# A two-layer metaformer kernel: one pass over a quadrant's similarity, seeds and inverse norms in place of two half passes

## The reference, cut to what matters

```python
x = x + _L0_conv_ref(_ln_c(x), ...)
# in _L0_conv_ref, for each quadrant (64 x 64 tokens) and head (4 heads of 24 channels):
sim = sigmoid(sim_beta + sim_alpha * einsum('bmc,bnc->bmn', _l2norm(ctr), _l2norm(pts)))
idx = argmax(sim, axis=1)                 # over the 4 centres, the first of equals
mask = (arange(M)[None, :, None] == idx[:, None, :])
sim = sim * mask
agg = (einsum('bmn,bnc->bmc', sim, value2) + value_centers) / (sum(sim, axis=-1) + 1.0)
out = einsum('bmc,bmn->bnc', agg, sim)    # then a 1x1 projection
```

## Time and profile before

| | |
|---|---|
| median of three runs | 3819.1 us |
| profiled execution | 3818.97 us |
| its span, first to last instruction | 3817.1 us |
| TensorE matmul busy, whole span | 2982.5 us (78%) |
| VectorE busy | 3196.7 us (84%) |
| ScalarE busy | 2886.1 us (76%) |
| POOL busy | 1726.6 us (45%) |
| mean granted TensorE clock, as a share of 2.4 GHz | 0.905 |

### The profile page before, as it was taken

How to read it: one execution, slowest core, us unless ns; L and a number is a source line. 1 busy time by engine, 2 the same in 40 slices (tenths; PEclk the granted TensorE clock), 3 DMA queues, 4 the chain that set the end, 5 groups by cost and what they waited for, 6 DMA issues and landing times. The chain is left out here.

```text
span 3817.1 us, 67552 instructions
## 1 busy us (share of the span) xinstructions
PE 2982.5 (78%) x21476; PEld 1982.1 (52%) x21476; DVE 3196.7 (84%) x8114; ACT 2886.1 (76%) x6562; POOL 1726.6 (45%) x2404
## 2 busy tenths in 40 slices
PE   5777777777777777777766999998878778778787
PEld 5556565656556565656543555554444444444443
DVE  4888888888888888888884899888898898889887
ACT  2577777777777777777776666665799999999998
POOL 3777777777777777777751000000221212221221
PEclk7798888888888888888876999999899999999999
DMA  2232323323332323333214777796666666666762
GB/s 59 59 84 68 84 68 84 84 76 84 76 84 67 84 68 84 81 79 85 59 52 130 216 219 220 220 281 177 162 184 190 171 176 192 187 169 175 195 178 67
DMA packets 708503, 484.58 MB, mean 127 GB/s; under 512 B 407068, under 2 KB 686940, under 8 KB 696156
## 3 DMA queue, kind: packets, MB, share of 16 engines
q1 hardware_dynamic: 708156, 480.27, 47.0%
HBM read 278.37 MB, written 201.33 MB: 126 GB/s over the span
## 5 line engine op out<-in xcount | busy, mean ns | idle before, releaser
L1834 POOL TENSOR_SCALAR C_var<-C_st 128x16 f32<-128x16 f32 x64 | 16.8, 263 | 1463.9 <-DVE C_st L175 1463.9
L1415 DVE SCALAR_TENSOR_TENSOR B_y<-B_mid,B_coefs,B_y 128x512 f32<-128x512 f32 x768 | 521.5, 747 | 77.4 <-ACT B_y L1382 77.4
L1333 PE MATMUL B_ps_row<-B_z,B_g 128*128 128x512 f32 x1152 | 520.1, 601 | 0.0
L375 DVE TENSOR_SCALAR A_hq<-A_h,A_b 128x512 f16<-128x512 f16 x768 | 292.5, 417 | 237.7 <-ACT A_h L367 230.7
L367 ACT ACTIVATE A_h<-A_hid 128x512 f16<-128x512 f32 x768 | 427.8, 593 | 63.4 <-PE A_hid L354 60.1
L175 DVE BATCH_NORM_STATS2 A_st<-A_xT 128x6 f32<-128x192 f32 x1536 | 443.3, 350 | 27.1 <-ACT A_xT L831 13.2
L367 ACT ACTIVATE C_h<-C_hid 128x512 f16<-128x512 f32 x768 | 426.7, 593 | 15.8 <-PE C_hid L354 8.6
L1455 ACT ACTIVATE C_q<-C_xT,C_shift,C_rstd 128x96 fp8e5<-128x96 f32 x1024 | 392.4, 458 | 30.7 <-POOL C_shift L1841 30.7
L861 ACT ACTIVATE A_xc<-A_xT,A_shift,A_rstd 128x96 f32<-128x96 f32 x1024 | 380.0, 459 | 0.0
L164 POOL TENSOR_TENSOR A_rstd<-A_var,A_expo 128x16 f32<-128x16 f32 x128 | 374.6, 2927 | 10.7
L668 PEld LDWEIGHTS A_fbank<-A_big_w,A_xq 97*128 97x128 f32 x2048 | 318.1, 225 | 29.2 <-issue 11.1
(11 more groups left out here) (160 smaller groups left out, 7325.8 us busy)
## 6 DMA issues: line engine op xcount, KB each, us to landing
A_xq<-in_x SPq DMA_DIRECT2D x32, 1536.0 KB, 8.9
x_scratch<-A_xT SPq DMA_DIRECT2D x64, 768.0 KB, 3.2
x_scratch<-A_x3h SPq DMA_DIRECT2D x64, 768.0 KB, 5.4
B_z<-x_scratch SPq DMA_DIRECT2D x96, 512.0 KB, 4.2
y_scratch<-B_y SPq DMA_DIRECT2D x96, 512.0 KB, 5.3
C_x3q<-x_scratch SPq DMA_DIRECT2D x32, 1536.0 KB, 9.1
C_xT<-x_scratch SPq DMA_DIRECT2D x64, 768.0 KB, 15.5
C_y3q<-y_scratch SPq DMA_DIRECT2D x31, 1536.0 KB, 15.5
```

What stands on the lines that cost most here:

```text
L375: r = dve.tensor_scalar(self.hq[:, b, s], self.h16[:, b, s], self.w["b1"][:, j:j + 1], 0.0, ALU.add, ALU.max)
L1333: m = pe.matmul(bank(c, h), g[c.buf(2)][:, d, :], z[c.buf(NB)][:, half(h), d:d + W], start=(d == 0), stop=(d == 2))
L1415: dve.scalar_tensor_tensor(y, mid[c.buf(2)][:, half(h), t:t + W], coefs[:, c.n, 3 + t:4 + t], y, ALU.mult, ALU.add).then_inc(ev["sums"], 1)
```

## The change

All of the quadrant's similarity is done at once. `cosines`, the sigmoid and `similarity` each run once for 128 x 128 (or 512) elements, in slots 5 and 6; the two transposes stand in slots 7 and 8; the seeds and the Newton steps run once, behind slot 3, with `pool_norm(i, 3)` ahead of them; `scaled_sim` runs once. The sums of squares are taken for two blocks at a time. The tie buffer becomes part of `eq`, whose rows grow from 4 to 9 floats: the running maximum of the marks stands in columns 0, 4 and 8, so the first copy falls away. `projected` writes its four diagonal blocks with one product by a mask of ones (`own_block`, four new columns of the constants).

```diff
-COS_AT = {3: 0, 5: 1}
-SIM_AT = {4: 0, 6: 1}
-SIMT_AT = {5: 0, 7: 1}
+COS_AT, SIM_AT = 5, 6
+SIMT_AT = {7: 0, 8: 1}
...
-        eq = sb("A_eq", [P, NT * HEADS, M], F32)
-        taken = sb("A_taken", [P, NT * HEADS, M - 1], F32)
+        eq = sb("A_eq", [P, NT * HEADS, M + (M - 2) * M - M + 1], F32)
...
-                pe.wait_ge(ev["sim"], ev.at("sim", q, h))
+                pe.wait_ge(ev["sim"], ev.at("sim", q, 0))
...
-                    act.wait_ge(ev["n2"], ev.at("n2", q, c - NSQ))
+                    act.wait_ge(ev["n2"], ev.at("n2", q, (c - NSQ) // 2))
...
-                        act.activation(sim[:, t, :], dots[:, t, :], ACT.Sigmoid, scale=ab[:, 0:1],
+                        act.activation(sim[:], dots[:], ACT.Sigmoid, scale=ab[:, 0:1],
...
-            def norms(q, c):
+            def norms(q, pair):
+                c = 2 * pair
-                dve.wait_ge(ev["big"], ev.at("big", q, c))
-                dve.tensor_reduce(n2[:, c * HM:(c + 1) * HM], sq[:, c % NSQ].rearrange("p t (h d) -> p (t h) d", d=HD),
+                dve.wait_ge(ev["big"], ev.at("big", q, c + 1))
+                dve.tensor_reduce(n2[:, c * HM:(c + 2) * HM],
+                                  sq[:, c % NSQ:c % NSQ + 2].rearrange("p k t (h d) -> p (k t h) d", d=HD),
                                   AX_X, ALU.add).then_inc(ev["n2"], 1)
...
-            def similarity(q, h):
+            def similarity(q):
...
-                dve.wait_ge(ev["eq"], ev.at("eq", q, h))
-                dve.tensor_copy(taken[:, u, 0], e[:, :, 0]).then_inc(ev["tie"], 1)
+                dve.wait_ge(ev["eq"], ev.at("eq", q, 0))
                 for m in range(1, M - 1):
-                    dve.wait_ge(ev["tie"], ev.at("tie", q, (M - 1) * h + m - 1))
-                    dve.tensor_tensor(taken[:, u, m], taken[:, u, m - 1], e[:, :, m], ALU.max).then_inc(ev["tie"], 1)
+                    if m > 1:
+                        dve.wait_ge(ev["tie"], ev.at("tie", q, m - 2))
+                    dve.tensor_tensor(eq[:, :, M * m], eq[:, :, M * (m - 1)], e[:, :, m], ALU.max).then_inc(ev["tie"], 1)
...
-                dve.tensor_tensor(e[:, :, 1:M], e[:, :, 1:M], taken[:, u, :], ALU.is_gt).then_inc(ev["only"], 1)
+                dve.tensor_tensor(e[:, :, 1:M], e[:, :, 1:M], eq[:, :, 0:M * (M - 2) + 1:M], ALU.is_gt).then_inc(ev["only"], 1)
...
-                for t in range(TPC):
-                    g = slice(32 * t, 32 * t + 32)
-                    m = dve.tensor_scalar(pabd[g, t * C:(t + 1) * C], s_pa[g, 0:C], rden[g, :], None, ALU.mult)
-                m.then_inc(ev["pabd"], 1)
+                dve.scalar_tensor_tensor(pabd[:].rearrange("p (t c) -> p t c", c=C),
+                                         s_pa[:, 0:C].unsqueeze(1).to_broadcast([P, TPC, C]), rden[:],
+                                         own_block.unsqueeze(2).to_broadcast([P, TPC, C]),
+                                         ALU.mult, ALU.mult).then_inc(ev["pabd"], 1)
...
-                for h in range(2):
-                    if q2.real:
-                        inverse_norms(q2, h)
-
-                        pool.wait_ge(ev["rn"], ev.at("rn", q2, h))
-                    if i.real and h == 0:
-                        ff.pool_norm(pool, i, 3)
+                if i.real:
+                    ff.pool_norm(pool, i, 3)
+                if q2.real:
+                    inverse_norms(q2)
                 if i.real:
                     ln3(i, 0)
-                if q2.real:
-                    scaled_sim(q2, 0)
                 if q1.real:
                     ln2(q1, 0)
...
                 if q2.real:
-                    scaled_sim(q2, 1)
+                    scaled_sim(q2)
```

More of the change, by code:

```diff
@@ L467, in phase_a @@
                     xT=NK, bn1=NK, ln1=2, ln1_s=4, pooled=1, cf=1, cfc=1, csq=1, cn2=1, cn2c=1, cpow=1, chat=1,
-                    c16=1, cw=1, cwc=1, big=NK, n2=NK, n2c=2, seed=2, rn_s=22, rn=2, guarded=2, cos=2, sig=2, mx=2, eq=2,
-                    tie=6, only=2, sim=2, simr=2, simT=2, side=1, sided=1, pool=1, agg=1, gathered=2, sum=1, summed=1, val=1,
+                    c16=1, cw=1, cwc=1, big=NK, n2=NK // 2, n2c=1, seed=1, rn_s=11, rn=1, guarded=1, cos=1, sig=1, mx=1, eq=1,
+                    tie=M - 2, only=1, sim=1, simr=1, simT=2, side=1, sided=1, pool=1, agg=1, gathered=2, sum=1, summed=1, val=1,
                     rden=1, aT4=1, pa=1, pabd=1, bn3=NK,
@@ L986, in cosines @@
[L986 to L992, removed]
+            def norms(q, pair):
[3 more added lines that the diff above has]
+                                  sq[:, c % NSQ:c % NSQ + 2].rearrange("p k t (h d) -> p (k t h) d", d=HD),
+                                  AX_X, ALU.add).then_inc(ev["n2"], 1)
+                if c + 2 == NK:
+                    dve.wait_ge(ev["n2"], ev.at("n2", q, pair))
+                    dve.tensor_scalar(n2c[:], n2[:], TINY, None, ALU.max).then_inc(ev["n2c"], 1)
+                    dve.wait_ge(ev["n2c"], ev.at("n2c", q, 0))
+                    dve.tensor_scalar(seed[:].bitcast(U32), n2c[:].bitcast(U32), -0.5, SEED_BITS, ALU.mult,
+                                      ALU.add).then_inc(ev["seed"], 1)
@@ new lines, in similarity @@
+                    dve.tensor_tensor(eq[:, :, M * m], eq[:, :, M * (m - 1)], e[:, :, m], ALU.max).then_inc(ev["tie"], 1)
+                dve.wait_ge(ev["tie"], ev.at("tie", q, M - 3))
+                dve.tensor_tensor(e[:, :, 1:M], e[:, :, 1:M], eq[:, :, 0:M * (M - 2) + 1:M], ALU.is_gt).then_inc(ev["only"], 1)
+                dve.wait_ge(ev["only"], ev.at("only", q, 0))
+                dve.tensor_tensor(sim32[:, :, 0:HM].rearrange("p t (h m) -> p t h m", m=M),
+                                  sim[:].rearrange("p t (h m) -> p t h m", m=M),
+                                  e.rearrange("p (t h) m -> p t h m", h=HEADS), ALU.mult).then_inc(ev["sim"], 1)
@@ L1061, in body @@
                         own_heads(q1)
-                    if q2.real and s in COS_AT:
-                        cosines(q2, COS_AT[s])
+                    if q2.real and s == COS_AT:
+                        cosines(q2)
                     if i.real and s < NK:
                         ff.dve_hidden(dve, i, s)
-                    for c in BIG_AT.get(s, ()):
-                        if q2.real:
-                            norms(q2, c)
+                    if q2.real and s in BIG_AT:
+                        norms(q2, s)
                     if i.real and s >= 1:
@@ L1085, in body @@
                         projected(q1)
-                    if q2.real and s in SIM_AT:
-                        similarity(q2, SIM_AT[s])
+                    if q2.real and s == SIM_AT:
+                        similarity(q2)
                     if q2.real and s == AGG_AT:
@@ L1886 @@
         consts[32 * t:32 * t + M, K_QUARTERS:K_QUARTERS + M] = np.eye(M, dtype=np.float32) / np.float32(2 * CH)
+    for t in range(TPC):
+        consts[32 * t:32 * t + 32, K_BLOCK + t] = 1
     consts[0:C, K_CEN:K_CEN + C] = np.eye(C, dtype=np.float32) - np.float32(1 / C)
```

76 lines of the change are left out of this document (31 added, 45 removed).

## The result

The changed kernel takes 3893.9 us (median of three runs, 3893.5 to 3895.6), the kernel before 3819.9 us beside it: a ratio of 1.0193, interval 1.0176 to 1.0210. A fourth run took 9402 us, a slow state that one later run of the kernel before shows too (6261 us); it counts in no number here. The change is slower by 74 us, where I had forecast 3822 us and a range up to 3848 us. The profiled execution took 3893.5 us, its span is 3891.7 us and the mean granted clock 0.882.

What follows compares the result with a forecast made beforehand. No one engine bounds the step throughout, though VectorE leads; -1.85 us (stretches A and B) and +1.9 (C) give +0.05 a step, 1.5 in 30 steps, plus 2 for filling: 3822 us from 3818.97, range 3790 to 3848.

Steps and rivals of the forecast that it cites:

- The mechanism: Bank order makes the gather's 64 matmuls wait for block 5's eviction, starting 2.04 us later; similarity once a step, about 3.5 us.
- One of its signs: Expected in the changed trace: VectorE's wait for the hidden copy grows by about what its busy time falls.
- Stretch C: Slot 8 to slot 1, a chain over all engines: the later gather makes it +1.9 us a step.
- I take half the steps at either level: Gather's clock: half the steps at 2.4 GHz, half at 1.2 GHz, so 7.58 - 5.67 = +1.9 us a step.
- Stretch A: Slots 2 to 4, ScalarE busy throughout: one sigmoid leaves, 0.5 us a step gained; VectorE's savings there worth nothing.
- Stretch B: From VectorE's wait for ScalarE's hidden copy to the end of slot 7's rounding: VectorE's savings count in full, -1.35 us a step.
- slots 0 to 1: The step's first two slots, from the first hidden copy to ScalarE's first copy of `y`: no size of their own forecast.
- The rival with the gather at half clock in every step: Gather at 1.2 GHz each time: +2.64 us from slot 8 on, step loses 0.79, 3845 us; chance 0.22.
- half clock that lasts into the next step's slot 0: TensorE's lower clock continuing past the hidden copy: left outside the range, with no size given.
- Filling the pipeline: Two quadrants pass with nothing beside them, longer instructions on the path: +2 us in all, bounds -2 and +6.
- the norm pairs and the masked product: VectorE's norm sums and `projected`, where ScalarE bounds: savings hidden, taken as nothing; norm pairs -0.2 to +0.2 us a step.
- POOL's Newton steps in a row: Twelve instructions of 128 elements, about 6.4 us between seeds and cosines with 9.5 us left: hidden, by 3 us.

Runs made afterwards that it cites:

- e1: The changed kernel with both transposes of the similarity in slot 7, so the gather no longer waits for block 5's eviction: 3772.1 us.
- e3: The changed kernel with 28 unread transposes ahead of TensorE's wait for the similarity in slot 7 and 8 behind it: 3839.9 us.
- e4: The kernel before with two parts of the change alone, norm sums by pairs of blocks and projected blocks by one masked product: 3826.1 us.
- e6: e1's kernel with the ties in a packed buffer of 12 bytes a row in place of 36, and one more copy: 3766.9 us.
- e10: e6's kernel with two parts undone, norm sums again block by block and projected blocks by four products: 3805.5 us.
- e9: e1's kernel with the gather's wait for the eviction of token block 5 put back: 3887.8 us.
- e5: e2's kernel with 28 plus 8 transposes in slot 7 whose results nobody reads: 3917.9 us.
- e7: The kernel before with 28 plus 8 transposes in slot 7 whose results nobody reads, no other edit: 3838.2 us.
- e11: e6's kernel without the copy of the first column; the first tie reads it in place, the last compare becomes two: 3777.0 us.
- e2: The kernel before with one wait added, the gather waiting for the eviction of token block 5 before its first matmul: 3990.4 us.

## Why the prediction was wrong

The mechanism was right: the wait for block 5's bank moved onto the gather, 27 times in the view; the similarity stands once a step. One of its signs was not: VectorE's wait for the hidden copy grew by 4.1 us a step, twice the 2.0 that its busy time fell. The forecast was +0.05 us a step; the table gives +2.47, 2.42 more. Four steps of the prediction failed, and no one of them makes the whole error: in C "I take half the steps at either level" (0.85 of the 2.42), in A the clock taken as fixed (0.58), in B what VectorE's savings come to (0.56), and slots 0 to 1, which have no term in the sum (0.42). By its steps:

- **Stretch C, +1.9 forecast, +2.75 measured.** The gather starts 5.10 us after slot 7's rounding where it was 3.07, 2.03 later (forecast 2.04); it takes 2.79 where it was 2.11 on the mean, +0.68; behind it +0.04. What failed is "I take half the steps at either level": all 26 ran at 1.2 GHz. The rival with the gather at half clock in every step had +2.64. TensorE's longer wait for the similarity (4.16 us at 1131.86) and the new wait (1.10) lie ahead of it; e1, without the second of these, has 2 long gathers, and e3, with TensorE kept busy through the first, none.
- **Stretch A, -0.5 forecast, +0.08 measured.** In the steps whose A ran at over 0.98 of the full clock the size came out: 16.95 us on the mean after, 17.56 before, -0.61 (1030.47 to 1047.43 above is one of them). But there are 7 such steps of 26 where there were 17, and the other 19 took 18.28. I had priced the clock where the wait stands, and taken it as fixed elsewhere. And the size is in part luck: e1, with the same work in A, took 17.65 us in its 10 such steps; 0.47 of that is POOL's normalisation, which there holds up slot 2's rounding (1.03 us on the mean in place of 0.56) and which the prediction had taken to be covered.
- **Stretch B, -1.35 forecast, -0.79 measured.** The similarity went from 2 x 2.595 to 3.67, -1.52 (forecast -1.7: ties 0.39 for 0.34, compare 0.67 for 0.57). The square at L967 takes 0.158 on the mean, -0.45 as forecast; the cosines +0.33 (+0.4); the ReLUs +0.47 (+0.4). Not in my sum: the roundings and the additions of the bias to `y` take 0.22 us longer. These parts come to -0.95; another 0.16 us stands in none of them.
- **Slots 0 to 1, not in the sum, +0.42.** A new collision, shown below. In e1, without it, this stretch is 1.35 us shorter than before, nearly all of it in TensorE's matmuls (busy for 7.94 us a step in place of 9.23, idle for 2.10 in place of 2.16), at a granted clock of 0.89 in place of 0.77. The prediction left "half clock that lasts into the next step's slot 0" outside its range without a price; the granted clock of this stretch did not fall (0.81, 0.77 before).
- **Filling the pipeline, +2 forecast (bounds -2 and +6), +7.9 measured** at the first of the copies above.
- **At nothing, and right:** the norm pairs and the masked product in the kernel before (e4; in e6's kernel they are worth 1.25 us a step, e10); POOL's Newton steps in a row and the seeds, as the waits of the changed kernel have no row in which VectorE waits for POOL.
- **Two readings that were off, at no cost to the sum:** not "nearly all" of VectorE's idle time was the wait for the hidden copy, but 182 of 250 us (from 200 to 1800 us); and 8 of 26 gathers took 2.79 us, not 10 of 27, though the mean of the stretch came out the same, since the others took 1.81 us on the mean, more than the 1.69 of the one shown.

The rival that came true is the gather at half clock, at 3845 us; it was too cheap because it carried A, B and slots 0 to 1 (1.56 us a step together) at what the main forecast had for them.

The slots 0 to 1: slot 0 of the step in order of time, of the kernel before and of the changed one.

```profile
1044.88 0.56 DVE L379 TENSOR_SCALAR A_hq<-A_hq 128x1536 uint16<-128x1536 uint16 x1
...
1046.28 0.17 DVE L1033 COPY A_summed<-A_fbank 97x16 f32<-97x16 f32 x1
...
1046.50 0.51 PE L708 MATMUL A_fbank<-A_summed,A_wv_ext 97*97 97x16 f32 x2 [2.17 <-DVE A_summed L1033]
```

```profile
1083.76 1.62 POOL L218 TENSOR_TENSOR A_xc<-A_xT,A_st 128x384 f32<-128x384 f32 x2
...
1085.34 1.97 POOL L227 TENSOR_TENSOR A_q<-A_xc,A_rstd 128x384 fp8e5<-128x384 f32 x2
1085.57 1.06 DVE L380 TENSOR_SCALAR A_hq<-A_hq 128x1536 uint16<-128x1536 uint16 x1
...
1087.41 0.16 DVE L1030 COPY A_summed<-A_fbank 97x16 f32<-97x16 f32 x1
...
1087.63 0.34 PE L708 MATMUL A_fbank<-A_summed,A_wv_ext 97*97 97x16 f32 x2 [2.98 <-DVE A_summed L1030]
```

Since the chain of C is late and POOL is not, POOL's products now start ahead of slot 0's rounding, which takes 1.06 us in place of 0.56 (the two roundings of this stretch take 2.01 us together on the mean, 1.12 before). Behind it the copy of the sums comes late, and TensorE stands 0.8 us longer. The same happens in the other kernels whose gather waits, e9 (1.06 and 0.87 us) and e5 (1.01 in slot 0); in e1, which differs from e9 by the wait alone, both roundings of this stretch take 0.56 and that of slot 2 takes 1.03.

What stays open: how the loss divides between the wait, the level of the clock and the collision. The gather's duration does not tell: in the kernel before, the 8 steps with a long gather take 9.51 us in C and 10.30 in the slots 0 to 1 behind it, the other 18 take 8.40 and 11.89, so that there what a gather at 1.2 GHz loses in C comes back behind it. Open is also what decides which stretch of a step gets the lower level. The runs show that it moves (e7, e10 and e11 shifted it into A, e1 and e6 out of slots 0 to 1), not why it goes where it goes.

## What to carry to other kernels

Where buffers are handed round in the order of use, one use moved later shifts the waits of all that follow; count off who gets which buffer, and ask whether the new wait stands ahead of a long group of matmuls or behind it. Here one place in the order, both transposes in slot 7, was worth 122 us (3894 to 3772). A wait on TensorE is not to be priced by its length: the granted clock can move in stretches far from it, so give the whole step's matmuls both levels in the range, and after an edit of a few tenths of a microsecond compare the clock by stretch before saying what the edit was worth.

## What the runs showed of the hardware

- A wait of 2.0 us on TensorE cost 6.33 us a step (e2), more than three times its length; the granted clock fell with it, in C from 0.74 to 0.53, in slots 0 to 1 from 0.77 to 0.67 and in A from 0.95 to 0.85.
- An edit that saved 0.16 us a step where it stands came out 10 us slower (e11), at the edge of what the runs can tell, with the granted clock of another stretch at 0.90 in place of 0.94.
- VectorE's ties, with two inputs of 32-bit floats, took 387 ns for 128 elements with all of them 36 bytes apart, and 388 with one input and the output 12 bytes apart and the other input 16; the compare of 384 elements took 674 ns in rows of 36 bytes with its second input 16 bytes apart, and 558 ns in packed rows. The Trainium skill (SBUF — State Buffer, "Door 1: The DMA port swizzle") has each access pay that goes to a new line of 16 bytes. By an estimate from that page every access at 36 or 16 bytes does so, and three in four at 12; the ties show no difference, though one of their inputs goes to a new line each time in either kernel. The compare is longer by a fifth, not doubled.
- VectorE's rounding, from 16-bit to 16-bit with one input, takes 0.56 us alone and 1.06 behind a running product of POOL. The Trainium skill (SBUF — State Buffer, "Who interferes with whom") has the two engines share a pair of ports, which in VectorE's two-port modes one of them holds for a whole instruction while the other is blocked. The trace agrees: a rounding that meets a running product of POOL ends 0.41 to 0.42 us after that product, whenever it began. That it runs in such a mode no run here shows.
